# A deformable convolution's gather table, written as vertical pixel pairs instead of four shifted copies

## The reference

```
gn     = group_norm(x)                        # 32 groups of 12 channels, per image
offset = clip(conv3x3(gn, off_w) + off_b, -8, 8)        # 18 numbers per pixel: y and x for 9 taps
mask   = 2 * sigmoid(conv3x3(gn, mask_w) + mask_b)      # 9 numbers per pixel
p[tap] = bilinear sample of gn at (pixel + tap + offset), 4 corner pixels, times mask[tap]
y      = sum over taps and channels of w[tap] * p[tap] + b
x      = x + gelu(batch_norm(y))
```

## Time and profile before

| | us |
|---|---|
| median of 3 runs | 3647.17 (3646.61 to 3649.19) |
| span of the profiled execution | 3649.7 |
| PE busy | 3328.9 (91%) |
| DVE busy | 2723.8 (75%) |
| ACT busy | 2248.0 (62%) |
| POOL busy | 1435.3 (39%) |

### The profile page before, as it was taken

The page is one execution under the profiler, slowest core; times in us unless marked ns, Lnnn a source line. Parts: engine busy times, 40 slices in busy tenths (PEclk is TensorE's granted clock), DMA queues, the critical chain, the costliest instruction groups (busy, mean ns, idle before and its releaser), DMA issues. The chain is left out here.

```text
span 3649.7 us, 61842 instructions
## 1 busy us (share of the span) xinstructions
PE 3328.9 (91%) x18190; PEld 1921.1 (53%) x18190; DVE 2723.8 (75%) x5169; ACT 2248.0 (62%) x5370; POOL 1435.3 (39%) x1536
## 2 busy tenths in 40 slices
PE   7969999999999999967999999968888888888897
PEld 3434444444444444456888888843444444444443
DVE  4468888888888788876888888845677676776766
ACT  3434444444444444455777777745887778787785
POOL 2134444444444444352222222221154453544535
PEclk9979999999999999998999999978999999999998
DMA  9999998898989899841000000011322322232221
GB/s 361 372 353 344 343 342 331 323 346 323 341 331 349 331 342 336 318 174 39 15 17 17 17 17 17 17 58 44 92 71 61 86 86 65 77 92 62 59 66 56
DMA packets 230542, 647.11 MB, mean 177 GB/s; under 512 B 31142, under 2 KB 127942, under 8 KB 229958
## 3 DMA queue, kind: packets, MB, share of 16 engines
q0 software_dynamic: 82944, 453.02, 33.2%
q1 hardware_dynamic: 147398, 191.91, 16.6%
HBM read 520.21 MB, written 79.18 MB: 164 GB/s over the span
## 5 line engine op out<-in xcount | busy, mean ns | idle before, releaser
L703 PE MATMUL b_acc<-b_sampled,b_w 128*128 128x512 f32 x2592 | 1215.3, 596 | 0.0
L638 DVE SCALAR_TENSOR_TENSOR b_mix<-shared,b_weight,b_mix 128x384 f32<-128x384 f32 x864 | 531.9, 621 | 139.6 <-ACT b_mix L661 81.9
L670 ACT ACTIVATE b_sampled<-b_tps 128x384 f32<-128x384 f32 x576 | 282.1, 490 | 572.8 <-PE b_tps L721 566.3
L703 PEld LDWEIGHTS b_acc<-b_sampled,b_w 128*128 128x128 f32 x2592 | 450.6, 192 | 348.9 <-issue 348.9
L1986 DVE TENSOR_REDUCE e_neg_top<-e_next 128x1 f32<-128x1024 f32 x384 | 469.8, 1224 | 193.4 <-PE e_next L2299 164.9
L638 DVE SCALAR_TENSOR_TENSOR b_mix<-b_got,b_weight,b_mix 128x384 f32<-128x384 f32 x864 | 531.3, 619 | 96.6 <-ACT b_mix L661 59.2
L2153 ACT ACTIVATE e_prob<-e_s 128x512 f32<-128x512 f32 x768 | 416.2, 597 | 128.4 <-PE e_s L2311 127.2
L2138 ACT ACTIVATE e_unused<-e_next,e_neg_top 128x1024 bf16<-128x1024 f32 x384 | 430.0, 1120 | 100.6 <-DVE e_neg_top L1986 100.6
L594 POOL DMA_INDIRECT shared<-corner_table,b_index x288 | 293.9, 1021 | 418.2 <-DVE b_mix L638 293.5
L594 POOL DMA_INDIRECT b_got<-corner_table,b_index x288 | 289.6, 1006 | 365.0 <-DVE b_mix L638 298.3
L721 PEld LDWEIGHTS b_tps<-ident,b_mix 128*128 128x128 f32 x1728 | 223.8, 142 | 372.1 <-issue 327.9
(11 more groups left out here) (230 smaller groups left out, 5367.0 us busy)
## 6 DMA issues: line engine op xcount, KB each, us to landing
corner_table<-y SPq DMA_DIRECT2D x32, 1536.0 KB, 14.9
e_stack<-e_high SPq DMA_DIRECT2D x384, 64.0 KB, 2.0
shared<-in_x SPq DMA_DIRECT2D x8, 1536.0 KB, 10.2
shared<-in_x SPq DMA_DIRECT2D x16, 768.0 KB, 5.8
tokens<-y SPq DMA_DIRECT2D x64, 192.0 KB, 1.9
e_tok<-tokens SPq DMA_DIRECT2D x8, 1536.0 KB, 7.9
e_stack<-e_low SPq DMA_DIRECT2D x192, 64.0 KB, 2.0
shared<-tokens SPq DMA_DIRECT2D x8, 1536.0 KB, 7.1
```

What stands on the lines that cost most here:

```text
L638: ins = nc.vector.scalar_tensor_tensor(dst[:], src[:, q * C:(q + 1) * C], weight[g][:, q, k, i:i + 1], dst[:], ALU.mult, ALU.add)
L670: nc.scalar.activation(sampled[s % 2][:, :, i * P:(i + 1) * P], tps[t % 2][:, 0:C].rearrange("p (o q) -> p o q", q=P), ACT.Copy).then_inc( ...
L703: last = nc.tensor.matmul(acc[g][co][:], w_conv[:, k, ci, co * P:(co + 1) * P], sampled[s % 2][:, ci], start=(k == 0 and ci == 0), stop=(k ...
```

## The change

A table row now holds two pixels: itself and the one below (2 x 384 floats, 3072 bytes). Two rows that follow each other hold all four corners, so a gather of 6144 bytes from row r reads rows r and r+1. Tokens are written twice for each image, not four times; the gaps are two transfers, not six. The corners come in another order in the gathered tile (the column pair is the outer index), so the weights are stored in that order. In `front`, the chunk pairs (0, 2) and (2, 0), which share no group of 12 channels, are left out: seven products, not nine.

```diff
-CORNER_SHIFT = [0, 1, SIDE, SIDE + 1]
-LEAD = SIDE + 1
+PAIR_SHIFT = [0, SIDE]
+PAIR = len(PAIR_SHIFT)
+LEAD = SIDE
...
-    table = nc.dram_tensor("corner_table", (BATCH * IMG_ROWS, CORNERS * C), F32, kind="Internal").ap()
+    table = nc.dram_tensor("pair_table", (BATCH * IMG_ROWS, PAIR * C), F32, kind="Internal").ap()
...
-        GAPS = 2 * (CORNERS - 1)
+        GAPS = PAIR
...
-                for s, d in enumerate(CORNER_SHIFT):
+                for s, d in enumerate(PAIR_SHIFT):
                     for first, many in ((0, LEAD - d), (LEAD - d + PIX, d)):
                         if many:
                             sp.dma_start(img_rows[first:first + many, :, s * C:(s + 1) * C],
...
                     sp.wait_ge(tp_free, TILES * (2 * j + u + 1) + 2)
-                    for s, d in enumerate(CORNER_SHIFT):
+                    for s, d in enumerate(PAIR_SHIFT):
...
-                    sp.wait_ge(table_written[u], 16 * CORNERS * BATCH // 2 + 1)
+                    sp.wait_ge(table_written[u], 16 * PAIR * BATCH // 2 + 1)
...
-                                    corner[u][:, g, 2 * a + b].rearrange("p k i -> p i k"),
+                                    corner[u][:, g, PAIR * b + a].rearrange("p k i -> p i k"),
...
-                    act.wait_ge(table_written[u], 16 * CORNERS * j + 1)
+                    act.wait_ge(table_written[u], 16 * PAIR * j + 1)
...
-                        for ci in range(CH):
+                        near = [ci for ci in range(CH) if abs(ci - co) <= 1]
+                        for ci in near:
                             last = nc.tensor.matmul(gps[:, 2 * co:2 * co + 2], same_group[:, ci, co * P:(co + 1) * P],
-                                                    stat[:, ci, :], start=(ci == 0), stop=(ci == CH - 1))
+                                                    stat[:, ci, :], start=(ci == near[0]), stop=(ci == near[-1]))
```

## The result

| | before | after |
|---|---|---|
| median of the runs made together, us | 3646.61 (3642.59 to 3650.28, 17 runs) | 3641.08 (3633.77 to 3650.3, 17 runs) |
| ratio after to before | | 0.9984, interval 0.9977 to 0.9992 |
| span of the profiled execution, us | 3649.7 | 3631.9 |

The changed kernel is faster by 5.8 us of 3647 (2.9 to 8.4); 3642.0 was forecast, within a range of 3636 to 3648. Two repeats of the same kernel gave 0.9986 (0.9976 to 0.9996) and 0.9979 (0.9969 to 0.9988). The two profiled spans differ by 17.8 us, three times as much as the medians: this pair of profiles can't be subtracted as a whole, and what follows compares marks within them.

A forecast was written before the change was run, and what follows sets the result against it. PE was taken to bound both stages; 4.15 us from seven products plus 1.0 us at the seam, all else zero, made 5.15 us off 3647.17, giving 3642.0 us, range 3636 to 3648.

The forecast's parts named there:

- PE bounds the loop of the first stage: First stage: PE's unbroken chain, not the full DMA engines, sets the period of 20.36 us an image.
- Seven products, 4.15 us: Group averages in `front`: four records less save 0.467 us in each of seven images, 0.88 us in the first.
- Nothing on PE waits for them, so inside the stage I cost this at nothing.: First stage's table writes, two for four: a third of the stage's bytes go, with zero gain inside the stage.
- The seam, 1.0 us: Between the two stages: last small writes land sooner once table writes drain early; gain 1.0 us, bounds 0 to 2.0.
- The gather costs nothing: Second stage's gathers: same packets, bytes and time despite the narrower table and overlapping reads; zero change.
- Cut at the rows: Slower rival, second stage: gather descriptors follow 3072-byte rows, 256 pieces each; 12 to 196 us lost, middle 104; chance 0.07.
- Nothing comes through: Rival, first stage: full DMA engines pace it, so the shorter `front` returns as waiting; time 3647; chance 0.11.
- Faster: Rival, second stage: gathers from the narrower table are served quicker, 14 us more saved, time 3628; chance 0.09.
- The 3 to 5 us that I allowed for the fetching of instructions: Whole kernel: changed instruction-list fetching could eat 4 to 5 us elsewhere, or shift the forecast some 3 us either way.

The follow-up runs named there:

- three writes: Changed kernel with one more table write per image, into a spare table nobody reads, three in all: 3639.07 us, ratio 0.997 to the kernel before.
- the shorter seam: Changed kernel with first image's index and weight tiles loaded inside the first stage, last table and places waits moved to the second: 3638.76 us, ratio 0.9974.

## Why the prediction was right, and where it was not

The time was right, and the mechanism for the larger part. That the forecast of 5.15 us lies so near the medians' 5.8 is in part luck: at the first mix the gain is 7.8 us, made of the products, a seam nearly twice as large as forecast, and 1.7 us of clock that no step had. Step by step:

- **PE bounds the loop of the first stage.** Right: the DMA share falls from 1.04 to 0.72, and the period only by what the products save.
- **Seven products, 4.15 us.** As a length right: 0.445 us an image for 0.467; 0.85 us for 0.88 in the first. I had divided the whole of a `front` by its records, but four records less took 2.10 to 1.66 us, 0.11 a record for my 0.117: a part of its time does not go with their number. 7 x 0.445 + 0.85 = 3.97 us. The statistics' start wanders by 0.2 us between executions and is none of it.
- **"Nothing on PE waits for them, so inside the stage I cost this at nothing."** This is the step that failed, though the total hid it. It was true of PE and not of the stage: the stage ends when SP has seen the last writes land, and the DMA engines' backlog was seen to end at about 198.9, 3 us after the corner weights that end PE's chain. With seven products alone, the offsets end 5.3 us earlier (184.47 and 185.34 for a mean of 190.17) and the seam grows from 5.1 to 10.2 us. I had the row for it, a wait of 1.3 us for the table at the seam with the engines at 0.72 until 199, and read it as a small cost of the seam. It was the sign that the transfers already ended last: a second limit next to the first. My working credited the 4.15 us to the products; they bring it only because the writes are fewer.
- **The seam, 1.0 us.** Too small: 1.8 us (means of three profiles each, 5.09 and 3.32). The upper end of my bounds, 2.0, came from the landing of a write in quiet, and that is nearly what was found. The last corner weights, 144 KB, land 4.0, 4.3 and 4.1 us after their issue in the three profiles before and 2.3, 2.4 and 2.3 us in the changed kernel, 1.8 us less in the mean. One profile of each, before first:

```profile
corner_w<-a_corner SPq DMA_DIRECT2D x1, 144.0 KB, 4.0
...
corner_w<-a_corner SPq DMA_DIRECT2D x1, 144.0 KB, 2.3
```

I had taken the middle of my bounds for the many small pieces of this write; in quiet they cost it no more than 0.4 us over the 1.9 us of the larger write. The Trainium skill, "DMA: Bandwidth & Descriptors", "Latency and other measured facts", gives the access latency of the chip's memory as 0.2 us on average and 2 us at high load. The difference of 1.8 us agrees with the seam here; the runs can't tell latency from a queue of earlier writes.
- **What no step had: 1.7 us of clock.** The kernel before has a fall to 1.2 GHz at 40 us in three profiles of three, at a cost of 1.7 us (7.91 for 6.21); seven products alone remove it (two of two), the table alone too (two of two), and none of the other seven profiles has it. Sum at the first mix: 3.97 + 1.70 + 1.77 + 0.34 for a gather that happened to land earlier = 7.78 us, for a measured 7.79. Why either edit removes the drop stays open.
- **The gather costs nothing.** Right: 82944 packets, 453.02 MB, 1.02 us an instruction, PE's idle time in front of L723 27.7 us for 27.9. The table is half as wide, neighbours overlap, and none of it shows.
- **The rivals.** "Cut at the rows" did not happen. Its price of 104 us, as the middle of 12 to 196, has a neighbour in the 166 us of two instructions with 128 pieces each; one instruction with 256 pieces, which is what the rival would have been, was not run. "Nothing comes through" was put down to engines that pace PE, for which there is no sign; but a kernel with half of the change does behave so, by the drain at the end. "Faster" had its 14 us in the gather stage; they are not there. The 3 to 5 us that I allowed for the fetching of instructions stood on no row, and no run shows them: the two queues of instructions moved 1.08 and 1.10 MB before, 1.08 and 1.09 MB after.

The medians show 5.8 us and the mark 7.8. The rest of the kernel, from the first mix to the end, took 3437.1 to 3440.8 us in three profiles before and 3430.1 to 3433.2 in three after, but 3440.9 with three writes and 3437.9 with the shorter seam, where the code from there on is nearly that of after. I can't book a part of it on the change; the 2 us between mark and median are inside the interval.

## What to carry to other kernels

- A stage that ends in a wait for transfers has two clocks running: the engine's chain and the backlog of its transfers. Compare both ends before you credit either edit; a wait for a transfer at the seam, even of 1 us, means that the transfers already end last, and then shortening the engine's work alone can buy nothing. Here the one edit brought 0.1 us at the first mix, the other 3.3, and both together 7.8.
- To find how far a full resource is from binding, add or take single pieces of load: one write of four less freed the whole seam, and the next one nothing, at a share that still read 0.93.
- Spans of two profiles can differ by three times the real gain. Marks early in the timeline, repeated over a few profiles, resolve 1 us where medians of ten runs resolve 3. A mark on one engine's list is not the start of the block: look for waits ahead of it (here 1.2 us on SP).

## What the hardware showed that I had not expected

- An indirect transfer of 128 pieces costs POOL 0.95 us and 0.30 us to the next when it does not wait, with pieces of 6144 and of 3072 bytes alike. In two gathers a step, the queue had 92160 packets for 1152 instructions, 80 each: 64 + 16 for 128 pieces, where pieces of 6144 bytes made 128 + 16. If the 16 are the same in both, pieces of 3072 bytes travelled two to a packet.
- The granted clock fell in the middle of unbroken PE work, behind a row of 18 short group-average records, in one kernel of the eight and there every time.
- SP's time for the same write depends on the queue: two table writes took 2.58 us, four took 14.45.
